# A Mamba block beside a mixture of experts: four PSUM banks for decays and states, four for products, and each product with C one scan later

## The reference

```python
dt = softplus(x_dbl[..., :16] @ dt_proj_w.T + dt_proj_b)      # (2, 2048, 512)
A = -exp(A_log)                                               # (512, 16)
def step(h, ts):
    dt_t, B_t, C_t, u_t = ts
    dA = exp(dt_t[..., None] * A)
    h = h * dA + (dt_t * u_t)[..., None] * B_t[:, None, :]
    y = einsum('bds,bs->bd', h, C_t)                          # sum over 16 states
    return (h, y)
y = ys + xc * D ; y = y * silu(z) ; y @ out_proj_w.T
```

## Time and profile before

| what | value |
|---|---|
| median of 3 runs | 1502.13 us (1500.19 to 1502.46) |
| the profiled execution | 1497.43 us, its span 1495.6 us |
| PE busy | 1240.6 us (83%) |
| DVE busy | 1242.4 us (83%) |
| POOL busy | 1203.2 us (80%) |
| ACT busy | 896.0 us (60%) |
| mean granted TensorE clock | 0.919 |

### The profile page before, as it was taken

How to read it: one execution, slowest core, us unless ns; L and a number is a source line. 1 busy time by engine, 2 the same in 40 slices (tenths; PEclk the granted TensorE clock), 3 DMA queues, 4 the chain that set the end, 5 groups by cost and what they waited for, 6 DMA issues and landing times.

```text
span 1495.6 us, 17205 instructions
## 1 busy us (share of the span) xinstructions
PE 1240.6 (83%) x4966; PEld 903.1 (60%) x4966; DVE 1242.4 (83%) x1547; ACT 896.0 (60%) x1972; POOL 1203.2 (80%) x638
## 2 busy tenths in 40 slices
PE   3874474689989887989998997999898998979977
PEld 2641121477567666766676766875776676746556
DVE  6599875599977997889988996999889998878834
ACT  4642443486756866676866765776767574645432
POOL 0444888798898889988899889998999799987740
PEclk8586886799999999999999999999999999979989
DMA  5774443678687757877698757886888578466640
GB/s 174 259 291 130 159 150 129 229 242 270 164 305 230 238 163 243 292 218 247 173 312 260 237 170 268 271 238 201 252 300 252 182 227 301 146 202 211 217 132 28
DMA packets 131518, 325.79 MB, mean 218 GB/s; under 512 B 15176, under 2 KB 29904, under 8 KB 120928
## 3 DMA queue, kind: packets, MB, share of 16 engines
q1 hardware_dynamic: 112224, 272.91, 54.0%
q0 software_dynamic: 13056, 41.95, 12.2%
q10 hardware_dynamic: 6144, 9.83, 1.8%
HBM read 259.75 MB, written 39.71 MB: 200 GB/s over the span
## 4 chain that ended last, share of the span: by engine, by line
POOL 30%; issue 25%; PE 18%; DVE 10%; ACT 4%; DMA 2%; SPq 0%; POOLq 0%; DVEq 0%; ACTq 0%
PE prod L1034 13%; POOL hxc L760 13%; POOL dbu L749 10%; DVE state L1419 7%; POOL slot_x L736 4%; DMA late<-moe 2%; PE prod L1086 2%; PE prod L1221 1%; POOL hxc L768 1%; PE prod L1222 1%; DVE hxc L1387 1%; POOL dtu L788 1%; ACT state L836 1%; POOL dt L781 1%; DVE prod L1432 1%
## 5 line engine op out<-in xcount | busy, mean ns | idle before, releaser
L1419 DVE TENSOR_TENSOR_SCAN state<-state,carry,dbu 128x512 f32<-128x512 f32 x512 | 657.6, 1284 | 126.6 <-ACT state L836 77.7
L749 POOL TENSOR_TENSOR dbu<-dtu,bb 128x1024 f32<-128x1024 f32 x256 | 628.4, 2460 | 50.3 <-DVE state L1419 43.7
L760 POOL TENSOR_TENSOR hxc<-hxc 128x1024 f32<-128x1024 f32 x155 | 375.1, 2420 | 95.9 <-DVE hxc L1387 95.6
L1387 DVE TENSOR_TENSOR hxc<-state,cb 128x512 f32<-128x512 f32 x512 | 353.8, 691 | 38.9 <-DVE state L1419 1.9
L836 ACT ACTIVATE state<-dt,par 128x512 f32<-128x512 f32 x512 | 352.6, 692 | 54.3 <-DVE hxc L1387 39.7
L1034 PE MATMUL prod<-late 128*128 128x256 f32 x1136 | 271.1, 396 | 47.7 <-DMA late<-moe 30.0
L1034 PE MATMUL prod<-xsT,late 128*128 128x256 f32 (+1 forms) x1280 | 265.8, 362 | 25.6 <-issue 19.5
L1034 PEld LDWEIGHTS prod<-late 128*128 128x128 f32 x1136 | 228.5, 204 | 86.4 <-issue 57.6
L1034 PEld LDWEIGHTS prod<-xsT,late 128*128 128x128 f32 x1280 | 222.7, 193 | 73.2 <-issue 39.7
L1086 PE MATMUL prod<-hxc,ident 128*128 128x512 f32 x212 | 123.0, 712 | 59.8 <-DVE hxc L1387 55.6
L834 ACT COPY carry<-state 128x1 f32<-128x1 f32 x384 | 60.8, 158 | 156.7 <-DVE hxc L1387 149.0
(11 more groups left out here) (168 smaller groups left out, 1240.4 us busy)
## 6 DMA issues: line engine op xcount, KB each, us to landing
bb<-bc_rows SPq DMA_DIRECT2D x256, 256.0 KB, 6.0
cb<-bc_rows SPq DMA_DIRECT2D x256, 256.0 KB, 5.0
late<-moe SPq DMA_DIRECT2D x40, 1028.0 KB, 5.5
late<-moe SPq DMA_DIRECT2D x40, 1024.0 KB, 6.8
hxc<-hxc POOLq DMA_DIRECT2D x36, 512.0 KB, 7.7
slot_x<-xc SPq DMA_DIRECT2D x18, 512.0 KB, 5.9
xs<-slot_x SPq DMA_DIRECT2D x31, 256.0 KB, 5.6
slot_y<-ys ACTq DMA_DIRECT2D x31, 256.0 KB, 5.4
```

The source lines that it names most:

```text
L749: nc.gpsimd.tensor_tensor(dbu[:, v % 3, :, :], dtu[:, n % 2, 2 * h:2 * h + 2, :], b, ALU.mult).then_inc(dbu_ready, 1)
L760: nc.gpsimd.tensor_tensor(hxc[:, to, :, :], hxc[:, to, :, :], hxc[:, piece, :, :], ALU.add).then_inc(summed, 1)
L1387: nc.vector.tensor_tensor(hxc[:, buf, c, :], state[:, k % STATES, :], cb[:, v % 4, :], ALU.mult).then_inc(hc_ready, 1)
L1419: nc.vector.tensor_tensor_scan(state[:, k % STATES, :], state[:, k % STATES, :], dbu[:, v % 3, c, :], carry[:, n % 2, col(k):col(k) + 1], ...
```

## The change

Two constants: `BANKS` goes from 5 to 4 and `STATES` from 3 to 4. `BETWEEN` and the owed product go. The product of step k - 1 is now issued directly behind scan k, whatever other work stands at the step; at the last step both products follow. So the order scan k, product k, scan k + 1, product k + 1 becomes scan k, product k - 1, scan k + 1, product k. Other work of the step comes behind the product. `bank_uses` makes a new table for four banks, and the decay of step k waits for the product of step k - 4.

```diff
-BANKS = 5
-STATES = 3
+BANKS = 4
+STATES = 4
...
-BETWEEN = ("CV", "YE", "OU", "M2")
...
-            owed = []
-
-            def product():
-
-                if not owed:
-                    return
-                k = owed.pop()
+            def product(k):
+
                 v, c = k // 2, k % 2
...
             def do(kind, name, i):
-                if kind == "S":
+                if kind in "SL" or name[:2] in VECTOR_WORK or name in ("M201", "M211"):
                     chore(kind, name, i)
-                elif kind == "L" or name[:2] in VECTOR_WORK or name in ("M201", "M211"):
-                    if name[:2] not in BETWEEN:
-                        product()
-                    chore(kind, name, i)
-                    product()
...
                 elif kind == "S" and name == "STEP":
-                    product()
                     k, v = i, i // 2
...
-                    owed.append(k)
+                    if k:
+                        product(k - 1)
+                    if k == NK - 1:
+                        product(k)
```

## The result

The changed kernel is slower: a median of 1523.96 us (1517.54 to 1529.85 in 4 runs) against 1502.3 us (1500.19 to 1502.56 in 4 runs), ratio 1.0148 with a 95% interval of 1.0117 to 1.0178. The forecast was 1473 us with a range up to 1515. The profiled execution took 1517.54 us, its span is 1515.7 us; it is the fastest of the four.

What follows compares the result with a forecast made beforehand. DVE was taken to set the pace, PE and POOL some 10% behind. Middle -24.0, first block -3.5, last -3.2, ends +1 gave about -29 us: 1502.1 to 1473 us, range 1448 to 1515.

Steps and rivals of the forecast that it cites:

- Part 1: On DVE, a product behind a foreign scan starts sooner: 0.135 us saved on average at 457 products, 61.7 us.
- Part 5: One bank fewer for PE's results: later PE starts, 0 to 68 us in the middle, 8 taken; 5 last block, 1 ends.
- The prediction's sign for this: Would show the bank cost wrong: DVE's waits for decays up over 46 us, ACT waiting for PE ahead of them.
- Parts 3 and 4: POOL's sum and SP's C row load wait one scan longer: 0 to 20 us, 7 taken; 0 to 11, 4 taken.
- Part 2: Decay waits for product k - 4; its window shrinks from 3.95 to 3.68 us: 9 us at worst, 3 taken.
- The first block: DVE's saving of 7.4 us there partly lost while POOL sets the pace: 3.5 us kept.
- The third rival: Slower by PE's banks: 68 us of middle bank waits less 46 saved, 1524 us (1505 to 1530); chance 0.25.

Runs made afterwards that it cites:

- The halved products: Kernel before with 240 products made over 256 of 512 tokens: ratio 0.9859; with four product and four state banks, old order: 1.0029 against 1.0172 unhalved.
- the paired order: Changed kernel ordered scan 2v, scan 2v + 1, product 2v, product 2v + 1: ratio 1.0073; same order in the kernel before (five product, three state banks): 0.9973.
- the late waits: Kernel before, POOL's sum and SP's C row load each waiting for one product more: both 1.0243, POOL alone 1.0182, SP alone 1.0116.

## Why the prediction was wrong

**Part 1, the size on DVE: right in kind, too small.** 61.7 us were forecast, 84.8 came. Behind a foreign scan the product starts 1.19 us after it, 1.20 forecast, but the next scan follows after 0.59 and not 0.64.

**Part 1, what of it lies on the path: the step that failed.** The prediction read "it sets the pace" from the fact that DVE mostly runs without a wait, and put the saving of the middle blocks, 46.0 of the 61.7 us, into the sum in full. Its own rows did not say so: in the six middle blocks DVE is the least busy of the three (865.1 us against 869.6 and 877.1), so PE and POOL were not "some 10% behind", all three stood at 89 or 90%. The page of the kernel before has one more row that the prediction did not use, the chain of work that ended last, by engine:

```profile
POOL 30%; issue 25%; PE 18%; DVE 10%; ACT 4%; DMA 2%; SPq 0%; POOLq 0%; DVEq 0%; ACTq 0%
```

It is one chain only, and it changes from kernel to kernel (those with decays in SBUF left out, POOL has 11 to 36% and PE 12 to 39%), but DVE has at most 14% in any of them. The halved products say what a microsecond off DVE is worth: 20 of 64, 0.3, with five banks and with four. With 0.3 the term is some 26 us for the 84.8 that came; the paired order at four and four banks shows 15.

One stretch of the changed kernel shows a place where the saving is lost while nobody waits for a bank, first DVE, then ACT:

```profile
576.50 1.29 DVE L1407 TENSOR_TENSOR_SCAN state<-state,carry,dbu 128x512 f32<-128x512 f32 x1 [0.82 <-ACT state L835]
...
581.86 1.29 DVE L1407 TENSOR_TENSOR_SCAN state<-state,carry,dbu 128x512 f32<-128x512 f32 x1 [3.49 <-ACT state L835]
```

```profile
576.48 1.28 ACT L913 ACT_TABLE_LOAD   x1
577.77 2.01 ACT L913 ACTIVATE dt<-dt 128x1024 f32<-128x1024 f32 x2
...
579.84 1.28 ACT L835 ACT_TABLE_LOAD   x1
581.14 0.69 ACT L835 ACTIVATE state<-dt,par 128x512 f32<-128x512 f32 x1
```

ACT works here without a wait, on the softplus of the next block's dt between two decays, with a load of a function table (1.28 us) on either side. DVE waits 0.82 + 3.49 = 4.31 us for it; at the same place of the kernel before it waits 1.45 (its scan at 576.82). The sooner DVE comes, the longer it waits.

**Part 5, the bank: under-sized.** 8 us in the middle, 5 in the last block and 1 at the ends were taken, 14 in all, from a range up to 68; the bank alone costs 29.5. The stretch at 552 us was read rightly, to the instruction: PE waits there in the changed kernel. What failed was the step from that one stretch, where nothing reached DVE, to all others. The mean lead of 3.2 and about 2.2 steps hides its low end: by the kernel's own table, of the 380 uses of a bank in the middle blocks 2 stand no step behind their reader with five banks, and 15 with four. That ACT then stands at PE's result, with the next decay behind it in its queue, is what the rows of the run with one bank less show (ReLU 40.1 to 65.9 us, decays 77.7 to 109.5). The prediction's sign for this was a rise of over 46 us in the middle; in the changed kernel it is 42.

**Parts 3 and 4, POOL and SP: the size was right, with some luck.** 7 and 4 us were taken, 11 together; the changed kernel less the paired order with the same banks is 11, with 5 to 17 in the intervals. That neither queue has slack, and that a delay of both costs 38 us, is shown by the late waits; how the 11 us divide between the two is not.

**Part 2, the decays: borne out in its main point.** The fourth state bank gives 2.5 us under the old order, inside the noise, and 21 under the new: it only pays for the later product. The 3 us taken for the window's 0.27 were not measured by themselves. What the part left out is that a faster DVE waits longer for a decay that comes no sooner: with four product banks and the old order, where a decay has 0.27 us more, DVE waits 109.5 us for decays, and in the changed kernel 131.8.

**The first block** was to save 3.5 us and takes 6.0 more, counted from its first scan to that of the next block. With the bank alone taken away it takes 208.0 us, with the late product and five banks 199.6, where the kernel before has 200.8. So it is the bank that costs there, where the two SUM banks leave two to rotate; the prediction had put nothing for it in this block.

The sum with the measured terms, by the ratios: -15 for the order, +26 for the bank less what the state bank gives (1.0172), +11 for the late product: +22, as measured. The first term is the difference of the paired and the old order, and the last closes the chain of three differences, so the sum must come out: it is a partition and not a proof. The bank term and the halving were each measured without the others. The third rival named the mechanism of the bank and 1524 us. The mechanism was right; the number was luck, since it was 68 for the bank less 46 for the order, where 26 and 15 came, and had no term for the late product. It had 0.25, because its condition, 46 us of gain to be outweighed, was itself built on the gain in full. With 0.3 of it the bank would have decided at 2 to 3 us a block.

## What to carry to other kernels

When three engines are each at 90%, a microsecond taken off one of them is not a microsecond of time; here it was a third of one. Price it by a run that shortens that engine's work alone before buying it with a buffer of another engine. A result that is handed on one step later, in a kernel where each engine is one queue in fixed order, can cost at every queue that waits for it (here 28 us at POOL's and 19 at SP's for some 2 us of delay): all that stands behind the wait is late, not only the waiter.

## What the runs showed of the hardware

With its decay in SBUF the scan is slower than with the decay in PSUM: 2327 ns on average against 1284. Timeline of the kernel with decays in SBUF, first DVE, then POOL:

```profile
699.35 1.29 DVE L1424 TENSOR_TENSOR_SCAN state<-dec,carry,dbu 128x512 f32<-128x512 f32 x1
...
701.87 3.01 DVE L1424 TENSOR_TENSOR_SCAN state<-dec,carry,dbu 128x512 f32<-128x512 f32 x1
...
713.08 1.29 DVE L1424 TENSOR_TENSOR_SCAN state<-dec,carry,dbu 128x512 f32<-128x512 f32 x1
```

```profile
701.44 2.35 POOL L762 TENSOR_TENSOR hxc<-hxc 128x1024 f32<-128x1024 f32 x1 [1.99 <-DVE hxc L1389]
703.76 3.29 POOL L751 TENSOR_TENSOR dbu<-dtu,bb 128x1024 f32<-128x1024 f32 x1
```

Where POOL is idle, or within 0.1 us of its end, the scan takes 1.29 us (713.08, 699.35). The one at 701.87 starts while POOL's sum runs, until 703.79, and ends at 704.88, 1.1 us after it; POOL's form, issued at 703.76, takes 3.29 us in place of the 2.36 and 2.41 of the earlier trace rows. Each seems to wait for the other to finish. Over the whole kernel the 97 scans that overlap no add or multiply of POOL take under 1.4 us each, and all 373 longer ones overlap one. The Trainium skill, SBUF — State Buffer, section "SBUF: two separate sides", states this: an operation of DVE with two SBUF inputs and one of GpSimd that reads SBUF need the same port pair, and whoever starts first holds it for the whole instruction. The trace agrees in the stretch shown. The longest scans go beyond it: the one of 8.80 us at 513.80 starts 0.15 us after POOL issued a transfer, spans three operations of POOL in a row (514.26 to 521.50) and ends 1.1 us after the third; why POOL kept its turn that long is open. The products and the scans of the kernel before each read one operand from PSUM, and keep their 0.69 and 1.28 us beside a busy POOL.
